# A decoder layer's feed-forward, second phase: int8 activations become bfloat16 in a casting transfer of GpSimd's queue instead of in copies on ScalarE and VectorE

## What is computed

```python
def _act_fake_quant(x, clip_factor):
    scale = jax.nn.sigmoid(clip_factor) * jnp.max(jnp.abs(x)) / QMAX
    return jnp.clip(_ste_round(x / scale), -QMAX - 1.0, QMAX) * scale
...
xq = _act_fake_quant(x, clip_x[0])
gate = jnp.einsum('bsh,ih->bsi', xq, _weight_fake_quant(w_gate))
up = jnp.einsum('bsh,ih->bsi', xq, _weight_fake_quant(w_up))
h = _act_fake_quant(jax.nn.silu(gate) * up, clip_down[0])
return jnp.einsum('bsi,hi->bsh', h, _weight_fake_quant(w_down))
```

## Time and profile before

| | us |
|---|---|
| three runs | 1007.6, 1010.6, 1010.87 |
| median | 1010.6 |
| the profiled execution | 1008.16 |
| its span in the profile | 1006.4 |
| phase 2 in the span | 967.3 to 1006.4 |

### The profile page before, as it was taken

The page is one execution under the profiler, slowest core; times in us unless marked ns, Lnnn a source line. Parts: engine busy times, 40 slices in busy tenths (PEclk is TensorE's granted clock), DMA queues, the critical chain, the costliest instruction groups (busy, mean ns, idle before and its releaser), DMA issues. The chain is left out here.

```text
span 1006.4 us, 16988 instructions
## 1 busy us (share of the span) xinstructions
PE 890.3 (88%) x5867; PEld 440.3 (44%) x5867; DVE 718.1 (71%) x1477; ACT 602.9 (60%) x1118; POOL 301.0 (30%) x343
## 2 busy tenths in 40 slices
PE   4788899999999899999999898999999867858855
PEld 2424343455544533554445344553445434443334
DVE  3789866768776774787777838777672386778977
ACT  2234577746576577356775764656786524627876
POOL 1242235420421229214231192233411212204510
PEclk9879999999999999999999999999999976978979
DMA  5240111335222142102221233012200612013017
GB/s 161 92 131 20 54 52 56 71 64 80 83 79 65 42 143 80 47 17 78 84 81 44 85 101 85 28 41 94 84 13 23 199 44 91 24 55 133 1 38 255
DMA packets 80063, 76.03 MB, mean 76 GB/s; under 512 B 19324, under 2 KB 74236, under 8 KB 79980
## 3 DMA queue, kind: packets, MB, share of 16 engines
q1 hardware_dynamic: 74908, 71.41, 22.8%
q10 hardware_dynamic: 3456, 2.94, 0.9%
q0 software_dynamic: 1616, 0.58, 0.7%
HBM read 22.43 MB, written 13.13 MB: 35 GB/s over the span
## 5 line engine op out<-in xcount | busy, mean ns | idle before, releaser
L752 ACT ACTIVATE probs<-psum 128x512 f32<-128x512 f32 (+1 forms) x608 | 314.6, 577 | 182.3 <-PE psum L945 179.4
L1119 DVE CUSTOM_DVE_ANT_0 junk<-psum,mask 128x640 bf16<-128x640 f32 (+3 forms) x256 | 253.5, 1022 | 62.9 <-PE psum L909 61.0
L669 POOL TENSOR_SCALAR_AFFINE_SELECT probs<-probs 128x512 f32<-128x512 f32 x128 | 81.3, 638 | 392.6 <-ACT probs L752 392.3
L945 PE MATMUL psum<-q_stack,k_stack 98*128 98x512 bf16 (+3 forms) x768 | 188.7, 332 | 7.9 <-DMA q_stack<-max_rows 2.7
L970 PE MATMUL psum<-probs,v_sb 128*17 128x512 f32 (+3 forms) x1536 | 159.5, 493 | 3.8 <-POOL probs L669 3.4
L1115 DVE TENSOR_REDUCE rowmax<-psum 128x4 f32<-128x512 f32 (+2 forms) x96 | 97.4, 1044 | 62.9 <-PE psum L903 62.5
L909 PE MATMUL psum<-k_stack,q_stack 96*128 96x512 bf16 (+3 forms) x512 | 129.5, 347 | 6.1 <-DVE rowmax L1119 4.8
L945 PEld LDWEIGHTS psum<-q_stack,k_stack 98*128 98x128 bf16 x768 | 63.0, 98 | 138.2 <-ACT probs L752 80.7
L869 PE MATMUL psum<-xnT,wT 128*128 128x512 f32 x192 | 95.4, 630 | 1.6 <-ACT xnT L717 1.5
L796 PE MATMUL psum<-wT,xnT 128*128 128x256 f32 x384 | 90.0, 393 | 2.0 <-ACT xnT L717 1.9
L796 PEld LDWEIGHTS psum<-wT,xnT 128*128 128x128 f32 x384 | 75.1, 198 | 14.3 <-ACT xnT L717 2.3
(11 more groups left out here) (173 smaller groups left out, 1203.3 us busy)
## 6 DMA issues: line engine op xcount, KB each, us to landing
q_stack<-q_parts SPq DMA_DIRECT2D x192, 64.0 KB, 2.6
k_stack<-k_parts SPq DMA_DIRECT2D x192, 64.0 KB, 2.6
xq_stack<-xq_parts SPq DMA_DIRECT2D x168, 64.0 KB, 2.6
xn<-in_x SPq DMA_DIRECT2D x8, 512.0 KB, 4.9
res<-in_x SPq DMA_DIRECT2D x4, 1024.0 KB, 7.1
resid_hbm<-res SPq DMA_DIRECT2D x8, 512.0 KB, 2.6
resid<-resid_hbm SPq DMA_DIRECT2D x8, 512.0 KB, 4.6
out<-o_sb SPq DMA_DIRECT2D x7, 512.0 KB, 3.2
```

Of the source, the lines that this page charges most:

```text
L669: nc.gpsimd.affine_select(out=tile, in_=tile, compare_op=ALU.is_ge, fill=0.0, base=0, pattern=[[0, GH], [1, P]], channel_multiplier=-1).th ...
L752: nc.scalar.activation(probs[n % 2][:, heads * k:heads * k + heads, 0:cols], bank_a(s)[:, 0:heads * cols].rearrange("p (h n) -> p h n", h= ...
L945: last = nc.tensor.matmul(bank[:, cols * n:cols * n + cols], k_stack[:, slot, h, P * j:P * j + P], q_stack[:, slot, half, h, q0 - HALF * h ...
L1119: nc.vector.tensor_tensor_reduce(out=junk[D_STEPS.place(s) % 2][:, 0:keys], in0=bank_d(s)[:, 0:keys], in1=m.mask[:, T - keys:T], scale=1.0 ...
```

## The change

- Blocks 1 to 6: both copies are gone. GpSimd's queue issues one transfer for each, from `h8` (int8) to `hq` (bfloat16); it waits for the rounding and, from block 3 on, for the product of block n-3. TensorE waits for the transfer's landing (`hq_in`, one semaphore for each buffer).
- Three buffers of `h8` and of `hq` instead of two. The third `hq` is laid over the `xf` buffers of phase 1, which become one tensor.
- ScalarE rounds block after block; from block 4 on it waits for the transfer of block n-3.
- Block 7 is rounded in two halves. VectorE copies them to bfloat16, after its addition of block 5 and before the scaling of block 6. TensorE multiplies the first three tiles of all rows, then the last three by pairs of row tiles.

```diff
@@ -1165,7 +1165,7 @@
     DEEP = 3
 
 
-    MINE, BACK = 3, 2
+    MINE = 3
 
 
     with ExitStack() as ctx:
@@ -1176,9 +1176,10 @@
             return ctx.enter_context(nc.semaphore(name))
 
         hidden = sb("hidden", [P, NB, FT, HALF])
-        xf = [sb(f"xf{s}", [P, CC, HALF]) for s in range(DEEP)]
+        xf_all = sb("xf", [P, DEEP, CC, HALF])
+        xf = [xf_all[:, s] for s in range(DEEP)]
         x8 = [sb(f"x8_{s}", [P, CC, HALF], I8) for s in range(2)]
-        h8 = [sb(f"h8_{s}", [P, FT, HALF], I8) for s in range(2)]
+        h8 = [sb(f"h8_{s}", [P, FT, HALF], I8) for s in range(3)]
         xq = [sb(f"xq{s}", [P, CC, HALF], BF16) for s in range(3)]
         silu = [sb(f"silu{s}", [P, HALF]) for s in range(FT)]
         up = [sb(f"up{s}", [P, HALF]) for s in range(FT - MINE)]
@@ -1186,7 +1187,9 @@
         small = sb("small", [P, 16])
         gscale, uscale = sb("gscale", [P, FT]), sb("uscale", [P, FT])
         dscale = sb("dscale2", [P, C])
-        hq = [sb(f"hq{s}", [P, FT, HALF], BF16) for s in range(2)]
+
+        hq = [sb(f"hq{s}", [P, FT, HALF], BF16)[:] for s in range(2)]
+        hq += [xf_all[:].rearrange("p s c n -> p (s c n)").bitcast(BF16)[:, 0:FT * HALF].rearrange("p (i n) -> p i n", i=FT)]
         resid = [sb(f"resid{s}", [P, 4, C]) for s in range(2)]
         o_sb = [sb(f"o_sb{s}", [P, 4, C]) for s in range(2)]
 
@@ -1201,7 +1204,8 @@
         x_rounded, xq_done = sem("x_rounded"), sem("xq_done")
         gu_full, silu_done = sem("gu_full"), sem("silu_done")
         mine_done, theirs_done, h_maxed = sem("mine_done"), sem("theirs_done"), sem("h_maxed")
-        h_rounded, hq_act, hq_dve = sem("h_rounded"), sem("hq_act"), sem("hq_dve")
+        h_rounded, last_rounded, hq_last = sem("h_rounded"), sem("last_rounded"), sem("hq_last")
+        hq_in = [sem(f"hq_in{s}") for s in range(3)]
         down_done, o_scaled, o_done = sem("down_done"), sem("o_scaled"), sem("o_done")
         first_rounded, first_done = sem("first_rounded"), sem("first_done")
         last_down, last_scaled, last_done = sem("last_down"), sem("last_scaled"), sem("last_done")
@@ -1221,7 +1225,7 @@
             for n in range(2, NB):
                 if n >= 2 + DEEP:
                     sp.wait_ge(x_rounded, n - DEEP + 1)
-                sp.dma_start(xf[n % DEEP][:], m.normT_hbm[BLOCKS[n]]).then_inc(xf_in[n % DEEP], 16)
+                sp.dma_start(xf[n % DEEP], m.normT_hbm[BLOCKS[n]]).then_inc(xf_in[n % DEEP], 16)
             for n in range(2):
                 sp.dma_start(resid[n][:], m.resid_hbm[BLOCKS[n]]).then_inc(resid_in[n], 16)
             for n in range(NB - 1):
@@ -1242,6 +1246,11 @@
                 for i in range(MINE, FT):
                     pool.wait_ge(silu_done, FT * n + i + 1)
                     nc.gpsimd.tensor_tensor(hidden[:, n, i, :], up[i - MINE][:], silu[i][:], ALU.mult).then_inc(theirs_done, 1)
+            for n in range(1, NB - 1):
+                pool.wait_ge(h_rounded, n)
+                if n >= 3:
+                    pool.wait_ge(down_done, n - 2)
+                pool.dma_start(hq[n % 3], h8[n % 3][:]).then_inc(hq_in[n % 3], 16)
 
         @block.scalar
         def _(act):
@@ -1264,16 +1273,16 @@
             for half in HALVES:
                 nc.scalar.activation(h8[0][:, half, :], hidden[:, 0, half, :], ACT.Copy,
                                      scale=small[:, HINV]).then_inc(first_rounded, 1)
-            for n in range(1, NB):
-                if n == 2:
+            for n in range(1, NB - 1):
+                if n == 3:
                     act.wait_ge(first_done, 2)
-                if n > 2:
-                    act.wait_ge(hq_dve, n - 2)
-                nc.scalar.activation(h8[n % 2][:], hidden[:, n, :, :], ACT.Copy, scale=small[:, HINV]).then_inc(h_rounded, 1)
-                act.wait_ge(h_rounded, n)
-                if n >= 2:
-                    act.wait_ge(down_done, n - 1)
-                nc.scalar.copy(hq[n % 2][:, 0:BACK, :], h8[n % 2][:, 0:BACK, :]).then_inc(hq_act, 1)
+                if n > 3:
+                    act.wait_ge(hq_in[n % 3], 16 * ((n - 1) // 3))
+                nc.scalar.activation(h8[n % 3][:], hidden[:, n, :, :], ACT.Copy, scale=small[:, HINV]).then_inc(h_rounded, 1)
+            act.wait_ge(hq_in[(NB - 1) % 3], 16 * ((NB - 2) // 3))
+            for half in HALVES:
+                nc.scalar.activation(h8[(NB - 1) % 3][:, half, :], hidden[:, NB - 1, half, :], ACT.Copy,
+                                     scale=small[:, HINV]).then_inc(last_rounded, 1)
 
         @block.tensor
         def _(pe):
@@ -1307,7 +1316,7 @@
             def down(n, i, t):
                 rows = P if i < FT - 1 else FR
                 return nc.tensor.matmul(m.psum[:, 2 * (n % 4) + t // 2, C * (t % 2):C * (t % 2) + C],
-                                        hq[n % 2][0:rows, i, P * t:P * t + P], m.wdT[0:rows, i, :],
+                                        hq[n % 3][0:rows, i, P * t:P * t + P], m.wdT[0:rows, i, :],
                                         start=(i == 0 and t % 2 == 0), stop=(i == FT - 1 and t % 2 == 1),
                                         skip_group_check=True)
 
@@ -1320,17 +1329,19 @@
             for n in range(1, NB - 1):
                 if n >= 4:
                     pe.wait_ge(o_scaled, n - 3)
-                pe.wait_ge(hq_act, n)
-                pe.wait_ge(hq_dve, n)
+                pe.wait_ge(hq_in[n % 3], 16 * ((n + 2) // 3))
                 for i in range(FT):
                     for t in range(4):
                         last = down(n, i, t)
                 last.then_inc(down_done, 1)
             pe.wait_ge(o_scaled, NB - 4)
-            pe.wait_ge(hq_act, NB - 1)
-            pe.wait_ge(hq_dve, NB - 1)
+            pe.wait_ge(hq_last, 1)
+            for i in range(FT // 2):
+                for t in range(4):
+                    down(NB - 1, i, t)
+            pe.wait_ge(hq_last, 2)
             for k in range(2):
-                for i in range(FT):
+                for i in range(FT // 2, FT):
                     for t in range(2 * k, 2 * k + 2):
                         last = down(NB - 1, i, t)
                 last.then_inc(last_down, 1)
@@ -1411,17 +1422,10 @@
             nc.vector.reciprocal(small[:, HINV], small[:, HSC]).then_inc(h_scaled, 1)
             link(nc.vector.tensor_scalar(dscale[:], m.dscale_f[:], small[:, HSC], None, ALU.mult))
 
-            def cut_h(n):
-                dve.wait_ge(h_rounded, n)
-                if n >= 2:
-                    dve.wait_ge(down_done, n - 1)
-                nc.vector.tensor_copy(hq[n % 2][:, BACK:FT, :], h8[n % 2][:, BACK:FT, :]).then_inc(hq_dve, 1)
-
             for k, half in enumerate(HALVES):
                 dve.wait_ge(first_rounded, k + 1)
                 nc.vector.tensor_copy(hq[0][:, half, :], h8[0][:, half, :]).then_inc(first_done, 1)
             for n in range(NB - 1):
-                cut_h(n + 1)
                 dve.wait_ge(down_done, n + 1)
                 if n >= 2:
                     dve.wait_ge(o_stored[n % 2], 16 * (n // 2))
@@ -1430,6 +1434,11 @@
                 dve.wait_ge(resid_in[n % 2], 16 * (n // 2 + 1))
                 dve.wait_ge(o_scaled, n + 1)
                 nc.vector.tensor_tensor(o_sb[n % 2][:], o_sb[n % 2][:], resid[n % 2][:], ALU.add).then_inc(o_done, 1)
+                if n == NB - 3:
+                    dve.wait_ge(down_done, NB - 3)
+                    for k, half in enumerate(HALVES):
+                        dve.wait_ge(last_rounded, k + 1)
+                        nc.vector.tensor_copy(hq[(NB - 1) % 3][:, half, :], h8[(NB - 1) % 3][:, half, :]).then_inc(hq_last, 1)
             n = NB - 1
             dve.wait_ge(o_stored[n % 2], 16 * (n // 2))
             dve.wait_ge(resid_in[n % 2], 16 * (n // 2 + 1))
```

More of the change, by code:

```diff
@@ L1212, in block_input @@
         def block_input(n):
-            return m.xnT[:, :, HALF * n:HALF * n + HALF] if n < 2 else xf[n % DEEP][:]
+            return m.xnT[:, :, HALF * n:HALF * n + HALF] if n < 2 else xf[n % DEEP]
         HALVES = (slice(0, FT // 2), slice(FT // 2, FT))
```

## The result

The changed kernel is slower by a little: over 20 runs its median is 1010.86 us (1003.99 to 1015.69), against 1007.88 us (999.33 to 1012.78) of as many runs of the kernel before. The ratio is 1.0037, with a 95% interval from 1.0019 to 1.0055, that is 1.9 to 5.5 us. The profiled execution has a span of 1013.6 us.

A forecast was written before the change was run, and what follows sets the result against it. ScalarE's 3.84 us a block bounded phase 2, the last residual load its end; transfer engines would become the bound. Profiled 1008.16 plus 5.6 gave 1013.8, or 1016.2 with the median's 2.4; forecast 1015 us, range 1008 to 1026.

The forecast's parts named there:

- the sum: Last residual load of phase 2: 11.0 MB at 360 GB/s take 30.6 us, landing at 1006.6 instead of 1001.0, +5.6 us.
- What bounds: Phase 2: the transfer engines become the bound, 5.4 us a block against 3.84 before; plain-rate transfers as bound, chance 0.53.
- the signs that were named beforehand: Phase 2: residual loads 6 us and more, casts 5 to 7, share 0.95 or above (978 to 1003), products 4.5 to 5.5 apart.
- The price of a cast: Each casting transfer of blocks 1 to 6: 2.9 us fixed plus 2.2 us moving, priced by the bytes written.
- The rate: Casts, stores and residual loads of phase 2 move at 360 GB/s; 325 would give +8.9 us, 410 +1.9.
- Who waits: VectorE's additions wait for residual loads, which take 6 to 8 us with a cast between; VectorE idles there.
- TensorE's clock: After idling, TensorE takes 4.8 us a block instead of 2.88; hidden behind transfers except at the last block: +2, so 1017.
- First block: Block 1: TensorE waits for the cast until 978.2 instead of starting about 974.2, costing 4.0 us once.
- The two moves at the end: Block 7 rounded and copied by VectorE in halves, 1.9 us, TensorE's second half too: free while the last residual is in flight.
- Slow cast: Rival for the casts: type change at 180 GB/s, 4.4 us moving each, +18.7, 1027 to 1029 us; chance 0.20.
- Clean: Rival for phase 2: transfers overlap well, pace falls to 2.86 us a block, 1006 to 1009.6 us, not slower; chance 0.27.

The follow-up runs named there:

- the idle casts in the kernel before: Kernel before, all copies kept, plus six casting transfers on GpSimd's queue that nobody waits for: phase 2 44.5 us, ratio 1.0075 to the kernel before.
- the third profile: The changed kernel, unaltered, profiled a third time: phase 2 46.5 us, with two slow blocks of 5.41 and 4.66 us.
- the dummy products: Changed kernel with dummy 128 x 256 products on TensorE ahead of its waits for a cast: phase 2 43.8 us, ratio 1.0014 to the kernel before.
- its second profile: The kernel before, unaltered, profiled once more: phase 2 39.3 us.
- the plain transfers: Changed kernel with a plain bfloat16 transfer, 0.786 MB written, in place of each casting one: phase 2 46.3 us.
- early residuals: Residuals of blocks 2 to 6 loaded ahead of phase 2: changed kernel 40.0 us, ratio 0.9957; kernel before 37.8 us, 0.9964.

## Why the prediction was right

The forecast was 1015 us, in a range from 1008 to 1026, and slower with a chance of 0.66. The median is 1010.86 us, 3.0 above that of before by the same count of runs, 3.7 by the ratio. Of the 4.1 us of difference to my figure, 2.7 are in the starting point: I leaned on a median of 1010.6 from three runs, and over 20 it is 1007.88. From there I had added 4.4, or 5.6 by the sum itself; measured are 3.7 [1.9, 5.5]. The direction and the kind of cause were right. That the figure came so near is in part luck: terms that were too dear and terms that were too cheap offset each other, as follows, and phase 2 grew by 6.1 to 7.8 us, more than my 5.6, of which the whole shows 3.7.

**What bounds.** Right in kind: the transfer engines went from 0.83 to 0.93 of the time to 1.05 to 1.08, and the idle casts in the kernel before show that their traffic alone costs 5.4 us of phase 2. By the section "Issuing engines are not separate DMA queues" of the Trainium skill's page "DMA: Bandwidth & Descriptors" GpSimd's queue brings no bandwidth of its own; the trace agrees, with residual loads of SyncE's queue at 7.3 us in place of 4.5 beside six transfers of the other.

Of the signs that were named beforehand, two did not hold: the share was to stay at 0.95 or above up to 1003 and was 0.60 from 997 to 1001, and TensorE's products were to be 4.5 to 5.5 us apart and were 3.4 to 4.8. The transfer engines are not full to the end; the sum of bytes over a rate leaves out that the last loads are issued late.

**The price of a cast: too high.** I took 2.9 us fixed and 2.2 moving, 5.1. The first two land in 3.6 and 3.5. The GB/s of 973 to 983 in 40 slices of 0.25 us:

```profile
GB/s 0 0 0 172 442 467 418 442 393 418 393 0 0 0 319 442 418 393 393 393 492 324 328 385 381 389 389 459 295 164 147 295 311 402 369 467 451 434 442 467
```

The eight slices from 973.75 on sum to 0.786 MB: 1.9 us of moving at 393 to 467 GB/s, so the fixed part is 1.7 us. The median of the small transfers was the wrong row; the minimum of the same view, 2.0, was the near one. The sum itself did not use the 2.9: it had 1.5 us from issue to first byte and 0.8 behind the last, which stood on no row; the trace shows about 1.0 and 0.6. The Trainium skill's page "DMA: Bandwidth & Descriptors", section "Anatomy of one DMA", has 2.0 us plus the bytes at 436 GB/s, an estimate of 3.8 us in all for this size. The trace agrees, with 3.6.

**The rate: too low.** I used 360 GB/s for everything; over the full windows it is 353 to 415, 391 in the mean. By bytes alone, then, the last residual should have landed 28.2 us after the first movement rather than 30.6, and the sum would have been +3.2 us.

**What made up for it.** The last residual lands at 1008.13, 41.5 us after the start of the phase; before, 1001.0, which is 33.7 after it. That is 7.8 us more in place of 5.6, and in the third profile it is about the same. Two steps had it too cheap. *Who waits*: I named the residual loads, at 6 to 8 us (measured 4.3 to 10.0, median 6.5). I did not name the stores. `o_sb` has two buffers, the stores now land in up to 7.5 us, and VectorE waits 4.8 us for them, twice what it waits for the residuals of its whole blocks (2.4). *TensorE's clock*: I had it hidden but for the last block. It is on the chain at block 1, 4.58 us for 2.88, since all that VectorE and the stores do comes behind it, and the dummy products put it at some 2 us. ScalarE, too, waited for casts, 1.40 and 0.46 us before its last roundings, as they took 6 us and more; that is off the chain.

**First block.** I said that TensorE starts on it 4.0 us later. From the start of the phase it is 976.38 - 966.67 = 9.7 us against 974.6 - 967.3 = 7.3 before, and 7.2 in its second profile: 2.4 to 2.5 later. Of the 1.6 us less than I said, 1.2 are the change's, whose cast was 1.5 us cheaper and issued 0.3 later, and 0.4 the kernel before's: there the copies were done by 974.4, but TensorE was on block 0 until 974.6.

**The two moves at the end** were free as forecast: the last residual landed 2.94 us after VectorE had got through its copies and block 6.

**Slow cast** is refuted by the plain transfers. **Clean** did not come; not even with early residuals does the change get below the 39.2 us of before (40.0).

## What to carry to other kernels

A copy that an engine gives to a transfer is not gone but has moved to a resource with a load of its own: read the transfer share of the very stretch first, and count all bytes written until the last load that the end waits for. A quick test that needs no rewiring is to add the transfers idly to the unchanged kernel and see what slows down. And where a copy of 1.05 us became a transfer of 3.5 or more, TensorE waited for it somewhere in every version without dummy products, and often came back from the wait at half its clock. Moving loads out of the crowded stretch made either kernel faster, which the change did not.

## What was unexpected of the hardware

- A transfer that turns int8 into bfloat16 goes by the bytes it writes: 0.786 MB in 3.5 to 3.6 us, the same as a plain one of 0.786 MB.
- With transfers inside SBUF in the mix, the 16 engines held 400 GB/s and more over 4 us windows (415, 406, 404 in the changed kernel, 413, 400, 420 and 413 in the one before with idle casts); with stores and residual loads alone the most was 286 at a share of 0.93.
- TensorE's granted clock fell to the level of 1.2 GHz for a part of a block or more after waits of 1.55 to 4 us, but not after every one: behind 1.69 us in one profile (4.50 us for the block), not behind 1.79 in another (2.88), nor behind 2.68 before the last block in the second (3.09, as before the change), while the kernel before kept 1.00 through its waits of 0.8 to 1.1 us.
